# A sum over targets in a graph kernel: another padding, one tile per sum, and selections on another engine

## What is computed

```python
seg = edge_type * n + dst
agg = jax.ops.segment_sum(x[src], seg, num_segments=N_REL * n)
mean = agg.reshape(N_REL, n, -1) / jnp.maximum(cnt, 1.0).reshape(N_REL, n, 1)
h1 = jnp.einsum('rni,rio->no', mean, W_rel) + x @ W_root + b_rgcn
```

## Time and profile before

| | us |
|---|---|
| median of 3 runs (3791.4 to 3793.32) | 3793.22 |
| the profiled execution | 3791.21 |
| its span, first to last instruction | 3789.6 |
| mean granted clock of TensorE, share of full | 0.971 |

### The profile page before, as it was taken

How to read it: one execution, slowest core, us unless ns; L and a number is a source line. 1 busy time by engine, 2 the same in 40 slices (tenths; PEclk the granted TensorE clock), 3 DMA queues, 4 the chain that set the end, 5 groups by cost and what they waited for, 6 DMA issues and landing times.

```text
span 3789.6 us, 56202 instructions
## 1 busy us (share of the span) xinstructions
PE 3509.1 (93%) x17647; PEld 2879.3 (76%) x17663; DVE 1956.8 (52%) x2740; ACT 1804.7 (48%) x2929; POOL 1751.0 (46%) x1329
## 2 busy tenths in 40 slices
PE   8998769999889897599989999999999999989998
PEld 4654449999789896233336999999999999955598
DVE  7537788888434545899955333333333331023335
ACT  1117878888633222599972444444444444400021
POOL 6888887765300001677101444444444444367600
PEclk9999979999989998899999999999999999999999
DMA  3321123333323213211025777777777775589801
GB/s 110 96 67 27 36 51 77 97 79 81 94 100 103 88 42 105 82 42 42 35 82 174 231 224 220 229 218 210 220 221 227 224 224 149 136 289 305 259 15 67
DMA packets 327199, 509.49 MB, mean 134 GB/s; under 512 B 195219, under 2 KB 211658, under 8 KB 327076
## 3 DMA queue, kind: packets, MB, share of 16 engines
q0 software_dynamic: 59584, 185.70, 16.9%
q1 hardware_dynamic: 85412, 194.37, 15.3%
q10 hardware_dynamic: 182080, 127.88, 12.0%
HBM read 346.22 MB, written 123.73 MB: 124 GB/s over the span
## 4 chain that ended last, share of the span: by engine, by line
PE 40%; ACT 7%; POOL 5%; issue 3%; DVE 2%; DMA 1%; SPq 0%; POOLq 0%; DVEq 0%; ACTq 0%
PE ps L1948 31%; POOL work L2055 5%; ACT work L1305 4%; ACT ps L1296 3%; PE ps L1588 3%; PE ps L307 2%; PE ps L1936 2%; PE ps L299 2%; DVE work L1127 1%; PE ps L1242 1%; DVE work L1155 0%; ACT work L1315 0%; DMA ct<-x_d 0%; DMA work<-msg_d,ct 0%; PE ps L325 0%
## 5 line engine op out<-in xcount | busy, mean ns | idle before, releaser
L1948 PE MATMUL ps<-wsplit,xsplit 128*128 x6840 | 1212.8, 336 | 0.0
L1948 PEld LDWEIGHTS ps<-wsplit,xsplit 128*128 128x128 f32 x6840 | 1185.0, 188 | 0.2 <-issue 0.2
L1913 POOL TENSOR_TENSOR xsplit<-ct,xsplit 128x768 fp32r<-128x768 f32 x190 | 361.4, 1902 | 368.6 <-ACTq L1999 240.8
L1305 ACT ACTIVATE work<-ps,work 128x418 f32<-128x418 f32 x720 | 438.4, 632 | 107.3 <-PE ps L1215 101.7
L1880 DVE CAST wsplit<-wplain 128x768 fp32r<-128x768 f32 x204 | 137.7, 675 | 680.1 <-PE ps L1948 659.2
L1252 PE MATMUL ps<-hbuf,work 128*128 128x193 f32 x2400 | 454.7, 327 | 16.2 <-DVE work L1169 13.1
L1252 PEld LDWEIGHTS ps<-hbuf,work 128*128 128x128 f32 x2400 | 407.0, 190 | 44.0 <-issue 16.7
L1296 ACT ACTIVATE ps<-work,lr 128x418 f32<-128x418 f32 x720 | 431.4, 633 | 6.4 <-DMA work<-lrow_d 6.4
L1155 DVE SCALAR_TENSOR_TENSOR work<-work,cnt 128x1250 f32<-128x1250 f32 x240 | 349.7, 1457 | 133.8 <-ACT work L1305 131.4
L2004 ACT ACTIVATE ct<-ps,invs 128x768 f32<-128x768 f32 x190 | 171.8, 904 | 485.7 <-PE ps L1948 472.6
L1242 PE MATMUL ps<-work,hbuf 128*65 128x512 f32 x720 | 323.4, 532 | 37.8 <-DVE work L1155 36.0
(11 more groups left out here) (221 smaller groups left out, 4247.9 us busy)
## 6 DMA issues: line engine op xcount, KB each, us to landing
wplain<-in_L_gnn_W_rel SPq DMA_DIRECT2D x34, 2304.0 KB, 10.5
msg_d<-ct ACTq DMA_DIRECT2D x190, 384.0 KB, 2.6
work<-lrow_d SPq DMA_DIRECT2D x47, 625.0 KB, 3.9
feat_d<-work ACTq DMA_DIRECT2D x30, 386.0 KB, 2.6
hbuf<-feat_d SPq DMA_DIRECT2D x60, 193.0 KB, 2.5
gat_d<-work POOLq DMA_DIRECT2D x12, 960.0 KB, 5.3
xplain<-gat_d SPq DMA_DIRECT2D x30, 384.0 KB, 3.1
wplain<-x_d SPq DMA_DIRECT2D x20, 384.0 KB, 3.1
```

Source lines behind the costliest of these rows:

```text
L1305: act.activation(self.p[q % 3][:, c0:c1], ps[:, b, 0:c1 - c0], ACT.Exp, bias=self.l2[:, col:col + 1], scale=1.0 - SLOPE)\
L1913: g.tensor_tensor(xlo7[:, k % XW, :], xt7[:, k % 2].rearrange("p c n -> p (c n)"), xhi7[:, k % XW, :].bitcast(F32), ALU.subtract).then_inc ...
L1948: last = pe.matmul(ps[:, 4 + 2 * (u % 2) + h, 0:HALF], x[:, u, c * P:(c + 1) * P], w[:, bass.ds(base + (c * D + h * HALF), HALF)], start=( ...
```

## The change

The messages get an order of their own, beside the target order of the counting stage: blocks of targets padded to 128 messages instead of 512, MT = 166 tiles instead of BT = 196. `message_order` computes it on VectorE in the first phase from the position in the target order; row_d then holds two words for each place, the row of the message and its target in the block (-1 for padding). In the sum stage each tile is a sum of its own (TensorE writes each tile's product to one of BS = 4 pairs of PSUM banks, and VectorE adds each pair to hbuf), and the selections are made by ScalarE (`act_sum`), two tiles at a time, as relu(1 - (iota - target)^2). `message_owners` computes the block of each tile in the W_OUT stage. The old lines of the sum stage are in the listing above and left out here.

```diff
+MT = (E + NT * (P - 1)) // P
...
-        row_d = dram("row_d", (P * BT, 1), I32)
+        row_d = dram("row_d", (P * MT, 2), I32)
...
+        mends = small[:, 48:48 + NT]
...
+            act.wait_ge(s_addr, 2)
...
+                if g == 1:
+                    step(v.tensor_copy(mpos, pos))
...
+            def message_order():
+                totals = offs[:, 1, R:R + NT]
+                for a, shift in ((0, 7), (1, 7 + (GT - 1).bit_length())):
+                    ti, tf = padt[:, 0:NT], small[:, 0:NT]
+                    step(v.tensor_scalar(ti, totals, float((1 << shift) - 1), None, ALU.add))
+                    step(v.tensor_scalar(ti, ti, shift, None, ALU.arith_shift_right))
+                    step(v.tensor_copy(tf, ti))
+                    if a == 0:
+                        step(v.tensor_tensor_scan(mends, tf, tf, 0.0, ALU.add, ALU.max))
+                    step(v.tensor_tensor(mstart[:, a, :], mends if a == 0 else ends[1], tf, ALU.subtract))
+                move = mstart[:, 0, :]
+                step(v.scalar_tensor_tensor(move, mstart[:, 1, :], -float(GT), move, ALU.mult, ALU.add))
+                for b in range(NT):
+                    step(v.tensor_scalar(mpart, fbuf[:, 1, :], float(b), move[0:EP, b:b + 1], ALU.is_equal, ALU.mult))
+                    step(v.scalar_tensor_tensor(mpos, mpart, float(P), mpos, ALU.mult, ALU.add))
+                step(v.tensor_copy(ibuf[:, 0, :], mpos))
+                step(v.tensor_scalar(ibuf[:, 1, :], ibuf[:, 0, :], P - 1, None, ALU.bitwise_and))
+                step(v.tensor_scalar(ibuf[:, 0, :], ibuf[:, 0, :], 7, None, ALU.arith_shift_right))
+                step.count(v.scalar_tensor_tensor(kept, ibuf[:, 1, :], float(MT), ibuf[:, 0, :], ALU.mult, ALU.add))
+                step.count(v.tensor_copy(msgpay[:, :, 0].bitcast(I32), row0))
+                step(v.tensor_copy(msgpay[:, :, 1], rec[:, :, 1]))
...
-            step.count(v.tensor_copy(kept[:, 0, :], addr[:, 1, :]))
-            step(v.tensor_copy(kept[:, 1, :], row0))
+            message_order()
...
+            step(g.memset(padmsg, 0.0))
+            step(g.memset(padmsg[:, :, 1], -1.0))
...
-        diff = c2(GT * P, BF16).rearrange("p (u n) -> p u n", u=GT)
+        diff = mask1[:, 0:GT * P].rearrange("p (u n) -> p u n", u=GT)
...
+        message_dst = drec[0:1, 192:192 + MT].bitcast(I32)
+        def message_owners(v, step):
+            owner = drec[0:1, 0:MT]
+            step(v.memset(owner, 0.0))
+            for b in range(NT):
+                step(v.scalar_tensor_tensor(owner, iota[0:1, 0:MT], mends[0:1, b:b + 1], owner, ALU.is_ge, ALU.add))
+            step(v.tensor_scalar(message_dst, owner, float(NT - 1), None, ALU.min))
...
+                    message_owners(v, step)
...
-        rows8 = c7(BT, I32)
+        rows8 = drec[:, 400:400 + 2 * MT].bitcast(I32)
...
+        MS, SS, BS = 16, 8, 4
...
+        diff8 = c8(4 * P).rearrange("p (q u n) -> p q u n", q=2, u=2)
...
         def pool_sum(g, step):
...
+            for t in range(MT):
+                if t >= MS:
+                    g.wait_ge(s_sum8, t - MS + 1)
+                g.indirect_dma_start(out=mg8[:, t % MS, :], out_offset=None, in_=msg_d,
+                                     in_offset=bass.IndirectOffsetOnAxis(rows8[:, 2 * t:2 * t + 1], 0)).then_inc(s_g8[t % MS][0], 16)
...
         def pe_sum(pe):
...
+            def tile(i, u):
+                t = MS * i + u
+                pe.wait_ge(s_sel8, (MS // 2) * i + u // 2 + 1)
+                if not isinstance(t, int) or t >= BS:
+                    pe.wait_ge(s_add8, t - BS + 1)
+                landed, before = s_g8[u]
+                pe.wait_ge(landed, before + 16 * (i + 1))
+                for h in range(2):
+                    last = pe.matmul(ps[:, 2 * (u % BS) + h, 0:HALF], sel8[:, u % SS, :], mg8[:, u, h * HALF:(h + 1) * HALF], start=True, stop=True)
...
+            for u in range(MS):
+                tile(0, u)
+            with pe.Fori(0, MT // MS - 1) as i:
+                for u in range(MS):
+                    tile(i + 1, u)
+            for t in range(MT // MS * MS, MT):
+                tile(t // MS, t % MS)
+        def act_sum(act, step):
+            def select(i, q):
+                at = 2 * SS * i + 2 * q
+                pair = SS * i + q
+                if not isinstance(pair, int) or pair >= SS // 2:
+                    act.wait_ge(s_sum8, at - SS + 2)
+                if not isinstance(pair, int) or pair >= 2:
+                    act.wait_ge(s_sel8, pair - 1)
+                for w in range(2):
+                    step.count(act.activation(diff8[:, q % 2, w, :], iota[:, 0:P], ACT.Square,
+                                              bias=local8[:, bass.ds(2 * (at + w) + 1, 1)], scale=-1.0))
+                step.wait()
+                u = 2 * q % SS
+                act.activation(sel8[:, u:u + 2, :], diff8[:, q % 2], ACT.Relu, bias=ones[:, 0:1], scale=-1.0).then_inc(s_sel8, 1)
...
+            for q in range(SS // 2):
+                select(0, q)
+            whole = (MT // 2 - SS // 2) // SS
+            with step.loop(whole, 2 * SS) as i:
+                for q in range(SS):
+                    select(i, SS // 2 + q)
+            for q in range(whole * SS + SS // 2, MT // 2):
+                select(0, q)
         def dve_sum(v, step):
...
+            def add(i, u):
+                t = BS * i + u
+                b = v.value_load(message_dst[0:1, bass.ds(t, 1)], min_val=0, max_val=NT - 1)
+                v.wait_ge(s_sum8, t + 1)
+                z = halves(hbuf[:, bass.ds(b * D, D)])
+                step(v.tensor_tensor(z, ps[:, 2 * u:2 * u + 2, 0:HALF], z, ALU.add))
...
+            with step.loop(MT // BS, BS) as i:
+                for u in range(BS):
+                    add(i, u)
+            for t in range(MT // BS * BS, MT):
+                add(t // BS, t % BS)
...
+            act_sum(act, step)
```

More of the change, by code:

```diff
@@ L445, in build @@
         scans = [mask1[0:EP, :].bitcast(F32)[:, 0:R * ET], ct1(NT * ET, parts=EP)]
-        kept = hbuf[0:EP, NT * (D + 12) - 2 * ET:NT * (D + 12)].bitcast(I32).rearrange("p (a t) -> p a t", a=2)
+        padmsg = ct1(MT * 2).rearrange("p (k c) -> p k c", c=2)
+        kept = hbuf[0:EP, NT * (D + 12) - 3 * ET:NT * (D + 12) - 2 * ET].bitcast(I32)
+        msgpay = hbuf[0:EP, NT * (D + 12) - 2 * ET:NT * (D + 12)].rearrange("p (t c) -> p t c", c=2)
+        mpos, mpart = c1(ET, F32, EP), c1(ET, F32, EP)
+        mstart = c1(2 * NT).rearrange("p (a n) -> p a n", a=2)
+        mends = small[:, 48:48 + NT]
         rows1 = ct1(2 * D).rearrange("p (u n) -> p u n", u=2)
@@ L2036, in act_rel @@
                 act.wait_ge(s_msgst[u], PLANES - 16 + 16 * (RT // 2 + 1))
[L2039 removed]
+        MS, SS, BS = 16, 8, 4
         c8 = Carve(work, WORK)
[L2041 removed]
+        mg8 = c8(MS * D).rearrange("p (u n) -> p u n", u=MS)
         assert c8.at <= 3 * KC * D
         c8(4 * KC * D - c8.at)
[L2044 to L2045 removed]
+        sel8 = c8(SS * P).rearrange("p (u n) -> p u n", u=SS)
+        diff8 = c8(4 * P).rearrange("p (q u n) -> p q u n", q=2, u=2)
+        local8 = drec[:, 400:400 + 2 * MT]
+        s_g8 = [(s, 3 * 16 * (ET // WAYS)) for s in s_scat] + [(sem(f"message_tile_in{u}"), 0) for u in range(MS - WAYS)]
         s_idx8, s_sel8, s_sum8, s_add8 = (sem(n) for n in ("indices8", "selected8", "summed8", "added8"))
@@ L2058, in pool_sum @@
             g.drain()
         def pe_sum(pe):
[L2061 to L2068, removed]
-                        last = pe.matmul(ps[:, 2 * (u % 2) + h, 0:HALF], sel8[:, GT * (u % 2) + w, :],
-                                         mg8[:, GT * u + w, h * HALF:(h + 1) * HALF], start=(w == 0), stop=(w == GT - 1))
-                last.then_inc(s_sum8, 1)
@@ L2073, in pe_sum @@
-            for k in range(UP):
-                group(k, k, 1)
-            with pe.Fori(0, BG // UP - 1) as i:
-                for u in range(UP):
-                    group(UP * i + UP + u, u, i + 2)
-            for k in range(BG // UP * UP, BG):
-                group(k, k % UP, k // UP + 1)
-        def dve_sum(v, step):
-            def select(k, u):
-                if not isinstance(k, int) or k >= 2:
-                    v.wait_ge(s_sum8, k - 1)
-                v.tensor_tensor(sel8[:, GT * u:GT * (u + 1), :], iota[:, 0:P].unsqueeze(1).to_broadcast([P, GT, P]),
-                                drec3[:, bass.ds(GT * k, GT), 1].unsqueeze(2).to_broadcast([P, GT, P]), ALU.is_equal).then_inc(s_sel8, 1)
-            def add(k, u):
-                b = v.value_load(group_dst[0:1, bass.ds(k, 1)], min_val=0, max_val=NT - 1)
-                v.wait_ge(s_sum8, k + 1)
-                t = halves(hbuf[:, bass.ds(b * D, D)])
-                step(v.tensor_tensor(t, ps[:, 2 * u:2 * u + 2, 0:HALF], t, ALU.add))
-                v.sem_inc(s_add8, 1)
-            for k in range(2):
-                select(k, k)
-            for k in range(2):
-                add(k, k)
-                select(k + 2, k)
```

(8 more changed lines are left out.)

17 lines of the change are left out of this document (6 added, 11 removed).

## The result

The changed kernel takes 3879.99 us (median of 4 runs, 3872.51 to 3883.26) where the kernel before takes 3793.2: a ratio of 1.0228, interval 1.0207 to 1.0248. It is slower by 87 us. A fourth run of the kernel before took 5027.1 us, a third longer than any other of it, and is left out of this comparison. The profiled execution took 3872.51 us and has a span of 3870.9.

The account below looks back on a forecast made before the run. TensorE bound the sum stage before; VectorE's adds, 2.02 us each, would bound it after. Stage +78.3 and extra copy +0.3 on 3791.2 give 3869.8, plus 2.0 to the median: 3872 us, range 3838 to 3893.

Parts of the forecast that it names:

- VectorE's serial add: Sum stage: load, address, add and its own wait follow one another on VectorE, 2.02 us each, above TensorE's 1.29.
- first gather to first add: Start of the sum stage: gather at 3330.07 us, first add at some 3340.7, 10.6 us in all.
- one add to the next, mean: Sum stage: 0.96 add, 0.88 unrolled gap, 0.09 branch share and 0.09 register arithmetic make 2.02 us (1.84 to 2.11).
- ahead of the stage: Before the sum stage: the extra copy of pos in the first sort delays the counts by 0.3 us.
- The branch: End of VectorE's loop of four adds in the sum stage: charged 0.35 us once in four adds.
- The unrolled gap: The last three counting-stage adds start 0.88 us after the previous one ends; taken as the gap between the new adds.
- the register arithmetic of the loop: Sum stage loop: about 0.09 us charged to each add for a register operation of 0.053 us and its issue.
- What was costed at nothing: Message order (at most 16 us), message owners (5 us) and ScalarE selections (under 1 us a tile): all expected hidden.
- covers: Existing waits expected to hide added work: 47.65 us for weights, 12.75 for a bias, 7.6 until the first tile lands.
- The adds keep up: Sum stage rival: loads overlap adds, TensorE keeps the pace, 39 us less, 3754 us; chance 7%.
- point of decision: Sum stage: 1.55 us an add; below it the change is faster than the kernel before, above it slower.
- The clock falls: Sum stage rival: pauses drop TensorE to 1.2 GHz, 2.56 us a tile, 89 us more, 3961 us; chance 5%.

Follow-up runs that it names:

- third trace of the kernel before: The kernel before run once more with nothing edited, to look for a held scatter: 3794.9 us (one run).
- the kernel with the body of sixteen: Changed kernel with each next owner's load issued beside the running add, in a loop body of sixteen adds instead of four: 3766.15 us, ratio 0.9921 to the kernel before.
- the second trace of the kernel before: The kernel before run once more with nothing edited, to look for a held scatter: 3803.7 us (one run).

## Why the prediction was right

*Direction and mechanism.* It forecast that VectorE's serial add sets the pace, against an engine that is busy a third of the time and waits 172 us. The trace shows it, doubling the load confirms it, and taking the load off the path undoes it. The 3872 us forecast is 8 under the median, 0.2%. For the profiled execution the sum gave 3869.8 us and 3872.5 were measured; that nearness is luck, since the stage is 7.0 us longer than forecast and begins 5.1 us earlier than forecast.

*The terms.*

| term, us | predicted | measured |
|---|---|---|
| first gather to first add | 10.6 | 10.0 |
| one add to the next, mean | 2.02 | 2.066 |
| sum stage | 344.9 | 351.9 |
| ahead of the stage | +0.3 | -4.8 in this execution |
| behind the stage | 0 | +0.8 |

The step that is mis-sized is the price of one add, by 0.046 us, 7.6 us in 165. The branch was charged at 0.35 us in four adds and costs 0.30. The unrolled gap carried over exactly: the last add, which stands behind the loop, starts 0.88 us after the one before it, as in the earlier trace rows. What failed is the register arithmetic of the loop, 0.09 us, read from one operation in the earlier trace rows. The changed kernel's sequencer, from 3443.9 to 3446 us, at the lines of the load and of the wait:

```profile
L2157 DVEq FUSED_REGOPS  x2: 57/124/190, 3444.1 to 3444.6; - x2
```

```profile
L2158 DVEq ALU_OP  x1: 40/40/40, 3444.8 to 3444.8; - x1
```

And the load's line for the two unrolled adds, 3674 to 3677.5 us, where the wait's line has no operation:

```profile
L2157 DVEq FUSED_REGOPS  x2: 190/190/190, 3674.0 to 3675.9; - x2
```

In the loop there is one operation for the load's index (57 ns; the other, of 190, follows the load, in unrolled code too), and another for the wait's value (40 ns), which in unrolled code is a constant. They are all that lies between two adds in the loop and not in unrolled code; the value of `step`'s own wait is formed too (L54, 40 ns at 3445.1 us), but beside the add. The gap is longer by 1.04 - 0.88 = 0.16 us; how it divides between the two and their issue no run shows. The prediction counted the index and forgot that the value of a wait inside a loop has to be formed as well.

*Ahead of the stage.* The 4.8 us earlier start can't be put down to the change. With the changed code ahead of it the stage begins between 3325.3 and 3342.6 us in eight traces, with the old code at 3330.1, 3333.2 and 3342.6 in three, and at the add of the earlier trace rows the third trace of the kernel before (1042.05 us) is level with the changed kernel (1042.17). Stage and rest alone, +85.3 + 0.8, give 3793.2 + 86.1 = 3879.3 us, within 1 us of the median.

*What was costed at nothing.* Rows of VectorE for the new order, the end of the counting stage, and the owners, against the earlier trace rows:

```profile
146.92 0.17 DVE L745 TENSOR_SCALAR work<-work 128x10 int32<-128x10 f32 x1 [0.15 <-DVE work L736]
...
158.65 0.30 DVE L761 COPY hbuf<-work 125x160 f32<-125x160 f32 x1
194.99 0.96 DVE L735 TENSOR_TENSOR work<-work,cnt 128x768 f32<-128x768 f32 x1 [36.05 <-DMA work<-in_L_gnn_W]
...
490.22 0.84 DVE L891 TENSOR_TENSOR ct<-hbuf,ct 128x1314 uint16 x1 [0.88 <-DVE ct L891]
...
1029.94 4.11 DVE L1478 SCALAR_TENSOR_TENSOR drec<-iota,small,drec 1x166 f32<-1x166 uint16 x10
1034.09 0.23 DVE L1479 TENSOR_SCALAR drec<-drec 1x166 int32<-1x166 f32 x1
1042.17 0.96 DVE L1515 TENSOR_TENSOR hbuf<-ps,hbuf 128x768 f32<-128x768 f32 x1 [7.84 <-DMA hbuf<-in_L_gnn_b_out]
```

The new order takes 146.92 to 158.95 us, 12 us where at most 16 were allowed, and the wait behind it shrinks from 47.65 to 36.05 us; its end moves from 194.44 to 194.99, within the 193.8 to 195.6 of the three traces of the kernel before, so that the 0.3 us charged for the extra copy can't be told. The last add of the counting stage starts at 490.22, not later than 493.01. The owners take 4.6 us and the wait behind them falls from 12.75 to 7.84. ScalarE's two squares and Relu were at most 1.5 us; they take 0.69 + 0.51. None of the covers was used up.

*What would show it.* 166 adds of 0.96 us came 2.0 apart with 1.04 idle before each. The releaser was named wrong: I expected the add before, the rows say "issue" (160 of 166). TensorE was to be busy 6 tenths and is 7.5, because a tile that stands alone takes 1.56 us from its first start to its last end, where its share of the full pipeline before was 1.29 us.

*The rivals.* "The adds keep up" is the right price of another kernel. Its point of decision, 1.55 us an add, was met nearly to the digit: at a mean of 1.544 us the time is that of the kernel before. What the 0.88 us would have had to lose for it was told too small, though: a third goes by the unrolled 1.84 us, and from the 2.02 us of the forecast it is 0.47 us, over half. Its 3754 us were reached (3751.57) once the load ran beside the add, the add raised the count itself and the body had sixteen adds. The Trainium skill's 125 ns (Perfetto Trace Analysis, Optimizing Scalar/DVE Operations) is the engine's own overhead on PSUM. No run here shows it by itself: with the load hidden or left out the gaps between adds were 0.21 us and more, waits for TensorE among them, and with the load between them 1.04. What bound the adds here was the sequencer, which that figure doesn't cover. "The clock falls" did not come: the granted clock is 1.00, 2.4 GHz, with TensorE busy 135.26 of 180 us and a pause after each tile, and in every run from 3400 to 3540 us, with the load doubled too, where TensorE is busy 80.66 of these 140 us. The swing that the Trainium skill tells of (TensorE: Matmul & The Clock Gate, A second HAM failure mode: psum-queue depth-cycling) is not seen in these stretches.

## What to carry to other kernels

The slack of an engine is not its idle time: ask what its sequencer does between two instructions, and look for unrolled code in the same trace that does just that, with nothing else between. An operation whose address is loaded, and that waits for itself before the next load, costs the sum of all these; issue the next load behind the operation and ahead of its wait, and let the operation raise the count itself. Here that brought an add from 2.07 us to TensorE's pace of 1.29. Before accumulating less in PSUM, multiply the number of hand-overs by that sum and hold it against the pace of the engine that is to be relieved.

## What was not expected of the hardware

*A scatter held by a series of VectorE operations.* GpSimd's timeline in the kernel with the body of sixteen, and VectorE's beside it:

```profile
84.71 1.17 POOL L835 DMA_INDIRECT dstrec_d<-work  x1 [0.31 <-issue]
86.19 7.69 POOL L835 DMA_INDIRECT dstrec_d<-work  x1 [0.30 <-issue]
```

```profile
82.68 10.16 DVE L702 SCALAR_TENSOR_TENSOR cnt<-mask,work,cnt 125x160 f32<-125x160 f32 x34
```

One scatter takes 7.69 us where its neighbours take 1.17. It ends at 93.88 us, one microsecond after the series of 34 operations of 125x160 (82.68 to 92.84) that VectorE issues without a pause. The scatters beside the same series in the changed kernel's own trace were not held. In the second trace of the kernel before one is held beside another series, and the last add of the counting stage starts 6 us later than in the earlier trace rows:

```profile
49.97 7.58 POOL L801 DMA_INDIRECT dstrec_d<-work  x1 [0.30 <-issue]
```

```profile
49.76 7.45 DVE L671 TENSOR_SCALAR cnt<-work 125x160 f32<-125x160 f32 x34
...
499.16 0.84 DVE L857 TENSOR_TENSOR ct<-hbuf,ct 128x1314 uint16 x1 [0.88 <-DVE ct L857]
```

It occurs in three of eight traces of the kernels with the changed code ahead of the sum and in one of three of the kernel before; in those four the last add of the counting stage starts at 499.2 to 501.4 us, in the other seven at 489.9 to 493.0. Some of the spread from run to run comes from there. The series at 50 us took 7.45 us where the scatter was held and 8.58 to 8.62 in the other ten traces, which fits a delay on both sides; the series at 82 us takes 10.15 to 10.18 us either way. The Trainium skill (SBUF — State Buffer, Who interferes with whom) says that a VectorE operation with two inputs in SBUF shuts out a GpSimd operation that reads SBUF, for the length of the instruction, and that TENSOR_SCALAR, which ran beside the held scatter in the second trace of before, can do so in its two-port modes. The rows show a hold over the rest of a series, not over one operation of 0.3 us, and only now and then; the measurement decides, and that rule alone doesn't account for it. Why it strikes one scatter and not the next was not tried and stays open.

*The branch of VectorE's loop.* The rows of the loop's end, 3449.9 to 3452 us:

```profile
L70 DVEq ALU_OP  x1: 40/40/40, 3450.1 to 3450.1; - x1
L70 DVEq COMPARE_BRANCH  x1: 56/56/56, 3450.2 to 3450.2; - x1
L70 DVEq FUSED_REGOPS  x1: 85/85/85, 3450.4 to 3450.4; - x1
```

The three together make 0.18 us and cost 0.30 with their issue. The Trainium skill (Advanced Engine Details and Errata, Control Flow Timing) has some 108 ns for a compare-and-branch. The row here has 56 ns, and what the loop costs is the longer sum of 0.30 us.
